# Cross-attention passes: the turns of the first and the last chunk's rows alternate between two PSUM banks

## What is computed

```
xq = (1 + scale) * layernorm(x) + shift
q = xq @ Wq + bq ;  k, v = split(context' @ Wkv + bkv)
out = softmax(q @ k^T / sqrt(32)) @ v          # per head
x = x + out @ Wp + bp
u = (1 + scale2) * layernorm(x) + shift2       # input of the next stage
```

## Time and profile before

| | us |
|---|---|
| median of 3 runs | 3903.49 |
| lowest and highest run | 3900.64, 3904.45 |
| the profiled execution's own time | 3910.66 |
| its span, first to last instruction | 3908.9 |
| mean granted clock of PE in it, as a share of the full 2.4 GHz | 0.95 |

### The profile page before, as it was taken

The page is one execution under the profiler, slowest core; times in us unless marked ns, Lnnn a source line. Parts: engine busy times, 40 slices in busy tenths (PEclk is TensorE's granted clock), DMA queues, the critical chain, the costliest instruction groups (busy, mean ns, idle before and its releaser), DMA issues. The chain is left out here.

```text
span 3908.9 us, 50109 instructions
## 1 busy us (share of the span) xinstructions
PE 3628.2 (93%) x18828; PEld 2403.3 (61%) x18828; DVE 2226.6 (57%) x3964; ACT 1870.3 (48%) x3442; POOL 2132.5 (55%) x1063
## 2 busy tenths in 40 slices
PE   5699988999999999999999999968999969999999
PEld 2577766875555555555555554426777748888887
DVE  2466652266777777777777777614766633222222
ACT  1455552115666666666666666644556532111111
POOL 0456540005898888889888888865677520000000
PEclk8798888999999999999999999987999879999999
DMA  7655657755555555555555554444575661111110
GB/s 231 154 157 149 177 146 221 241 176 141 125 120 120 127 127 132 128 124 118 120 127 130 128 131 103 116 132 110 149 181 157 159 206 58 49 44 44 44 44 33
DMA packets 232009, 505.92 MB, mean 129 GB/s; under 512 B 38199, under 2 KB 55095, under 8 KB 211799
## 3 DMA queue, kind: packets, MB, share of 16 engines
q1 hardware_dynamic: 213335, 368.49, 34.6%
q0 software_dynamic: 18432, 134.23, 15.7%
HBM read 215.54 MB, written 144.51 MB: 92 GB/s over the span
## 5 line engine op out<-in xcount | busy, mean ns | idle before, releaser
L2117 DVE TENSOR_REDUCE first_peak<-first_sm 128x1 f32<-128x512 f32 x1963 | 1211.1, 680 | 358.7 <-PE first_sm L1947 357.5
L2077 ACT ACTIVATE a_e<-a_st 128x512 f32<-128x512 f32 x2048 | 1061.7, 603 | 534.7 <-PE a_st L1966 523.5
L2177 POOL TENSOR_TENSOR a_esum<-a_esum,a_e 128x2048 f32<-128x2048 f32 x256 | 1208.8, 4722 | 18.5
L1966 PE MATMUL a_st<-first_q,first_k 128*128 128x512 f32 x2048 | 825.5, 406 | 16.8 <-ACT a_e L2077 12.0
L1947 PE MATMUL first_sm<-first_k,first_q 96*128 96x512 f32 x1963 | 833.1, 424 | 0.0
L1947 PEld LDWEIGHTS first_sm<-first_k,first_q 96*128 96x128 f32 x1963 | 369.9, 188 | 425.2 <-DVE first_peak L2117 316.2
L1979 PE MATMUL a_acc<-a_e,a_v 128*32 128x512 f32 x4096 | 505.7, 600 | 0.0
L1966 PEld LDWEIGHTS a_st<-first_q,first_k 128*128 128x128 f32 x2048 | 387.6, 190 | 131.2 <-ACT a_e L2077 51.7
L2365 ACT ACTIVATE mlp_gelu<-mlp_ph,mlp_b 128x512 f32<-128x512 f32 x128 | 88.3, 690 | 590.0 <-PE mlp_ph L2327 590.0
L2419 POOL TENSOR_TENSOR mlp_x<-mlp_x,mlp_brow 128x2048 f32<-128x2048 f32 x8 | 39.5, 4934 | 581.7 <-DMA mlp_x<-s_x 581.7
L2327 PE MATMUL mlp_ph<-mlp_us,mlp_w_hi 128*128 128x512 f32 x1024 | 336.6, 391 | 19.2 <-DMA mlp_us<-s_u 19.2
(11 more groups left out here) (161 smaller groups left out, 5317.2 us busy)
## 6 DMA issues: line engine op xcount, KB each, us to landing
a_esum_moved<-a_e POOLq DMA_DIRECT2D x128, 1024.0 KB, 7.3
p_qs<-s_q SPq DMA_DIRECT2D x192, 256.0 KB, 5.9
s_q<-p_qo SPq DMA_DIRECT2D x64, 512.0 KB, 7.6
first_k<-s_k SPq DMA_DIRECT2D x24, 1024.0 KB, 11.0
first_q<-s_q SPq DMA_DIRECT2D x96, 256.0 KB, 7.1
s_x<-p_x SPq DMA_DIRECT2D x16, 1024.0 KB, 4.4
s_u<-p_ut_hi SPq DMA_DIRECT2D x64, 256.0 KB, 5.8
s_u<-p_ut_lo SPq DMA_DIRECT2D x64, 256.0 KB, 6.4
```

Source lines behind the costliest of these rows:

```text
L1966: pe.matmul(st[0:KR, place(kt, h) % RING], k[:, g % 2, h, kt * P:kt * P + KR], q[:, j % QR, h], start=True, stop=True).then_inc(score_done, 1)
L2077: act.activation(e[0:KR, (j * NKT + kt) % ER, h], st[0:KR, place(kt, h) % RING], ACT.Exp, scale=SCALE).then_inc(score_read, 1)
L2117: dve.tensor_reduce(dst, src, AX.X, ALU.max).then_inc(unit_read, 1)
L2177: pool.tensor_tensor(esum[:], e[:, slot(0)] if x == 1 else esum[:], e[:, slot(x)], ALU.add).then_inc(e_added, 1)
```

## The change

Eight turns of each pass get a fixed bank by a small function: those of the first chunk's query rows (which 1, n 0) and of the last chunk's u rows (which 2, n 7) go to `acc` for t = 1 and 3 and to `pt` for t = 0 and 2. All other turns stay in `pt`. A turn now waits for the reading of the last turn in the same bank, and ACT reads the turn's bank. Nothing else is changed: no instruction is added or removed, and no engine's order of work.

```
+        def turn_bank(which, n, t):
+
+            return acc if (which, n) in ((1, 0), (2, N - 1)) and t % 2 else pt
...
             def turn(which, n, t):
                 number = turns.index((which, n, t))
-                if number:
-                    which2, n2, t2 = turns[number - 1]
+                bank = turn_bank(which, n, t)
+                same = [other for other in turns[:number] if turn_bank(*other) is bank]
+                if same:
+                    which2, n2, t2 = same[-1]
                     pe.wait_ge(turn_read[which2], n2 * KT + t2 + 1)
                 for tt in range(TT):
                     if t == 0:
                         pe.wait_ge(xn_done[which - 1], n * TT + tt + 1)
-                    mm = pe.transpose(pt[:, tt * P:(tt + 1) * P], xn[:, tt, t * P:(t + 1) * P], ident[:])
+                    mm = pe.transpose(bank[:, tt * P:(tt + 1) * P], xn[:, tt, t * P:(t + 1) * P], ident[:])
                 mm.then_inc(turned[which], 1)
...
-                act.activation(hi, pt[:], ACT.Identity, bias=shift(b, t), scale=scale(b, t))
-                act.activation(full, pt[:], ACT.Identity, bias=shift(b, t), scale=scale(b, t)).then_inc(turn_read[which], 1)
+                bank = turn_bank(which, n, t)
+                act.activation(hi, bank[:], ACT.Identity, bias=shift(b, t), scale=scale(b, t))
+                act.activation(full, bank[:], ACT.Identity, bias=shift(b, t), scale=scale(b, t)).then_inc(turn_read[which], 1)
```

## The result

The changed kernel takes 3895.01 us, the median of 22 runs (3887.16 to 3904.39), against 3903.8 us for the kernel before, the median of 22 runs on the same chips (3893.48 to 3915.53). The ratio is 0.9979, with a 95% interval of 0.997 to 0.9987: 8.2 us less, between 5.1 and 11.7 us (the two medians themselves are 8.8 us apart). A second comparison on one chip, further down, gives 0.9984 (0.9973 to 0.9994), 6.2 us. The forecast was 7.4 us and 3896.1 us. These intervals are wide: both hold the forecast and also the sums of rival 1 (8.2 us) and rival 3 (10.2), and the second holds the 4.8 us of rival 2. The whole time alone can't choose between them.

The account below looks back on a forecast made before the run. PE, busy 93% of the span, bounds the long stages, so the change could matter only where PE waits. Terms 1.3 + 1.4 + 3.1 + 1.6 = 7.4 us off the median 3903.49 gave 3896.1 us, range 3891.5 to 3900.5.

Parts of the forecast that it names:

- rival 1: At the end of p1 the transfers keep pace and 3.9 us arrive: sum 8.2, time 3895.3 us; chance 0.20.
- rival 3: Clock rises earlier at both pass starts, winning 1.4 us twice: sum 10.2, time 3893.3 us; chance 0.10.
- rival 2: Stores hinder each other at both pass ends (sum 4.8 us), or starts lose to the clock (sum 6.1); chance 0.25.
- The ladder: At both ends of p1 and p3, PE's turns and ACT's reads alternate; each step falls from 2.65 to 1.34 us.
- the two splits: At the start of p3, two splits of another tile stand between ACT's reads, 0.66 us each.
- The starts: Query projection at the starts of p1 and p3 waits for POOL's fourth lo part; gains 1.3 and 1.4 us.
- The end of p1: Stores queue at 1.6 us a pair, so 3.1 us of ACT's 3.9 us gain arrive.
- The bound of 254 GB/s: Slow case for stores at the end of p1: 2.06 us a pair, gain only 1.2 us.
- The end of p3: Fourth hi read must wait in the three-place ring for the first turn's stores to land; gain 1.6 us, not 3.9.
- The clock: At both pass starts, a clock rise at an unmoved moment cuts the starts' gain from 2.7 to 1.4 us, sum 6.1.
- rival 4: Nothing arrives: passes' middle absorbs the starts' gain, barrier and loads the ends'; time 3902 to 3904 us; chance 0.05.
- Rival 5: In the passes' middle, over 16 us of additional low clock makes the kernel slower; 32 us give 3911 us; chance 0.05.

Follow-up runs that it names:

- the kernel with the old waits: Changed kernel's alternating banks, but each turn waits for ACT's reading of the turn ahead, whatever its bank; ratio 1.0006 to the kernel before, 12 runs.
- POOL's order: Changed kernel with the first chunk's bias rows behind POOL's four lo parts: 3898.3 us, one run; two profiles also gave p3's last fourth turn a free tile.

## Why the prediction was right, and where it was off

**The ladder.** A step was to fall from 2.65 to 1.34 us; it fell to 1.33. That the gain is the overlap and nothing else is shown by the kernel with the old waits. "3.9 us on ACT at each of the four places" holds at three of them; at the start of p3 it is 2.9, since the two splits no longer hide behind PE. The forecast named the splits but left the 3.9 as it was, and lost nothing by it only because POOL was the bound there.

**The starts.** 1.3 and 1.4 forecast, 1.34 and 1.42 measured. That POOL is the bound there is shown by moving the bias rows. What was said of them for p1, that 2.6 us of ACT's gain are lost to POOL, is the 2.60 us by which that kernel's start of p1 is shorter.

**The end of p1.** 3.1 forecast, 2.6 measured: the largest miss. The mechanism was right, since the stores queue and fewer bytes end it sooner. The size of one term was off: I took 1.6 us for a pair from pairs that stood alone, and back to back it is 1.8. The transfers thus took a little over 7.0 us and not 6.4, and where the sum gave the queue 0.8 of ACT's 3.9 us, it took 1.3 (5.98 us behind the last issue instead of 4.65). The bound of 254 GB/s was too slow. Its mean took in the slice with 193, in which the stores in flight were running out; the three slices ahead of it (217, 274, 332) have a mean of 274. The measured 295 GB/s lies between that and the 328 that 1.6 us a pair mean. Rival 1, in which the transfers keep pace (8.2 us), falls with it.

The estimate by the Trainium skill ("DMA: Bandwidth & Descriptors", section "Anatomy of one DMA"), 1.20 us a pair at 436 GB/s, falls too: a pair took 1.8 us here. That section's figures were fitted to transfers issued by GpSimd, which the prediction didn't say, and these stores are issued by SP.

**The end of p3.** 1.6 forecast, 1.5 measured, with the new wait at the place named. The landing took 3.2 us instead of 3.1, with the next pair behind it.

**The clock.** The rise behind the first query matmul was seen 2.7 to 6.1 us later in p1 and p3 of these profiles; 4.4 us in p1 and 6.1 in p3 before, 5.6 and 4.3 in the changed kernel. It didn't stay at a fixed place, and it didn't come within 1.5 us of the first query matmul as rival 3 needed in my working. The Trainium skill ("TensorE: Matmul & The Clock Gate", section "What's actually happening") says that the gate's window is free-running and doesn't reset with the kernel; these rises agree with that in so far as they keep no fixed place.

What such a rise costs can be read at the first scores. The times from ACT's first normalisation to them, mean and range over the profiles with the same start:

| start as in | profiles | p1, us | p3, us |
|---|---|---|---|
| before | 5 | 31.68 (31.28 to 32.18) | 31.67 (30.80 to 32.02) |
| changed | 5 | 29.71 (29.34 to 30.46) | 29.70 (29.40 to 29.98) |
| POOL's order | 3 | 27.64 (26.87 to 28.10) | 28.95 (28.89 to 29.02) |

The groups don't overlap, so the starts' gains do reach the first scores. Beside the change's 1.34 and 1.42 us these means fall by 2.0 each, and the rise came 1.2 us sooner behind the first query matmul (5.0 to 3.7 us in p1, 5.1 to 4.0 in p3). By the forecast's price of 0.47 us for each us of low clock that is worth 0.6 us, which is the difference. In the first two profiles alone the rise of p1 came 1.2 us later and that of p3 1.8 sooner, and 0.85 and 2.16 us arrived. Whether the rise tends to come sooner in the changed kernel or did so by chance is not shown.

**Do the starts' gains reach the end of the pass?** The forecast said so, and against it stood rival 4. The mean middle of p1 is 476.5 us in the five profiles with the old start, 473.2 in the five with the changed one and 469.6 in the three with POOL's order. The starts differ by 1.34 and 2.60. In p3 the means are 522.9, 519.5 and 521.6 (starts 1.42 and 1.50 apart). Within each group the middles spread by 2 to 8 us. So in p1 the middles speak for the gain arriving (the groups differ by more than it); in p3, and to less than some 2 us anywhere, they settle nothing. The timed ratios fit the sum of all four places each time (6.9 us forecasts 0.9982, measured 0.9979 and 0.9984; 12.2 us forecasts 0.9969, measured 0.9969 and 0.9966), which speaks for all of it arriving, with intervals some 4 us wide to each side. What is shown is the gain at the ends and, for the starts, the gain up to the first scores.

**Faster, same or slower.** I gave 0.40 to faster by over 0.2%. The measured 0.9979 is just beyond that bound and 0.9984 just within, with both intervals across it, so on which side the change lies is open. Rival 5, slower by more time at the low clock in the middle, didn't happen. Its counter-argument was weak all the same: three runs within 3.8 us seemed to speak against swings, and 22 runs of the same kernel lie 22 us apart. That the median of three came within 0.3 us of the median of 22 was luck, and the forecast of 3896.1 us rests on it.

## What to carry to other kernels

A pair of engines that hand one buffer back and forth shows as two brackets that name each other; a second buffer takes out the shorter half of each step, but only where no other work fills the gap, which here is at the ends of the pipelines. Follow the faster engine's output at once through every queue behind it: of 3.9 us at three places and 2.9 at the fourth, POOL's order, the bandwidth of the stores and a ring of three left 1.3 to 2.6, and moving one of POOL's steps gave more than the change itself had given there. Ask too what stood in the gap: work that was free while its engine waited has a price once the gap is closed. With single executions that differ by 10 us, judge a change of 7 us by the stretches that it touches, which repeated to 0.05 us in every profile, and keep the whole time for many runs.

## What the runs showed of the hardware

A pair of 256 KB stores with rows of 2 KB that stood alone moved in about 1.6 us (a mean of some 328 GB/s, single slices up to 385); four such pairs back to back averaged 295 GB/s, and this gap is where the forecast missed. From issue to landing a lone lo store took 3.1 to 3.2 us, and the four in the queue 3.3, 3.7, 4.2 and 4.6.

ACT's reads of one PSUM bank took 0.77 to 0.80 us in the changed kernel, with PE writing the other bank (573.11 and 575.77) and with PE idle (0.80 at 577.11), against 0.77 and 0.78 in the kernel before.

One program's middles, between the same instructions, differed by up to 7.1 us from one execution to the next (p3 before: 527.4 and 520.3), while its waits and durations at the pass ends agreed to 0.02 us. The executions' granted clock goes with their length. Of the 23 runs of the kernel before in the last comparison, the two with a mean clock of 0.948 have spans of 3910.1 and 3912.1 us, the two with 0.953 have 3894.0 and 3896.9. Full speed is 1.00 and half speed 0.50, so 0.005 of the span is 0.005 x 2 x 3900 = 39 us more at the lower clock, for 15.7 us more time: 0.4 us for each. The forecast's price was 0.47. Here too it is not shown what makes the clock differ from one execution to the next.
